# Adding expert outputs in memory with an accumulating scatter, in a fused attention and mixture-of-experts kernel

## The reference, cut to what matters

```
topk_w, topk_ids = grouped_topk(logits, bias)        # 6 of 64 experts a token
buf = zeros(E, CAP + 1, H).at[se, slot].set(x[tok])[:, :CAP]   # CAP = 48
h   = silu(einsum('ech,ehf->ecf', buf, w_gate)) * einsum('ech,ehf->ecf', buf, w_up)
out = einsum('ecf,efh->ech', h, w_down)
gathered = out[se, min(pos, CAP - 1)] * valid[:, None]
y = segment_sum(gathered * w, tok, num_segments=Tn)  # sum of a token's kept expert outputs
```

## Time and profile before

| | us |
|---|---|
| median of 3 runs | 516.87 (515.25 to 517.76) |
| span of the profiled execution | 517.1 |
| token stage, until the first pair's rows are there | 0 to 377 |
| pair stage | 377 to 464 |
| end stage | 464 to 517.1 |

### The profile page before, as it was taken

The page is one execution under the profiler, slowest core; times in us unless marked ns, Lnnn a source line. Parts: engine busy times, 40 slices in busy tenths (PEclk is TensorE's granted clock), DMA queues, the critical chain, the costliest instruction groups (busy, mean ns, idle before and its releaser), DMA issues.

```text
span 517.1 us, 7330 instructions
## 1 busy us (share of the span) xinstructions
PE 309.6 (60%) x2282; PEld 222.4 (43%) x2282; DVE 283.7 (55%) x1066; ACT 98.9 (19%) x253; POOL 212.8 (41%) x310
## 2 busy tenths in 40 slices
PE   0735695968678768859657867150089889940000
PEld 0424484856556556747445655040045444520000
DVE  3550516395194394393393392664067544727995
ACT  1411131413112212303113201000024332430000
POOL 4200112117517527327327237186615433553664
PEclk9958568896786886796787787655579865985555
DMA  7955992963411311311301300000059999119992
GB/s 224 399 183 178 260 317 71 239 214 127 171 35 61 125 47 47 122 41 39 122 20 38 122 22 8 0 5 2 3 153 300 277 270 228 57 38 379 333 323 96
DMA packets 62332, 73.63 MB, mean 142 GB/s; under 512 B 9458, under 2 KB 56955, under 8 KB 62304
## 3 DMA queue, kind: packets, MB, share of 16 engines
q1 hardware_dynamic: 41456, 53.37, 35.2%
q10 hardware_dynamic: 14704, 15.24, 8.4%
q0 software_dynamic: 6144, 4.66, 3.1%
HBM read 48.39 MB, written 40.93 MB: 173 GB/s over the span
## 4 chain that ended last, share of the span: by engine, by line
issue 27%; PE 19%; DVE 16%; POOL 15%; DMA 10%; another core or an unknown queue 5%; ACT 3%; SPq 2%; DVEq 1%; ACTq 0%; POOLq 0%
POOL rows_dram L449 8%; PE ps_s L1268 5%; DVE z L1019 4%; DMA h2row<-rows_dram 2%; DVE scm L821 2%; DMA xa<-in_L_attn_x 2%; DMA scm<-rows_dram 2%; DMA egu<-y_dram 2%; POOL rstd L435 2%; PE ps_o L1166 2%; SPq L300 1%; PE ps_o L1281 1%; PE ps_a L1257 1%; PE ps_c L1281 1%
## 5 line engine op out<-in xcount | busy, mean ns | idle before, releaser
L449 POOL DMA_INDIRECT rows_dram<-h2row,slot_ix x96 | 94.3, 983 | 28.1 <-issue 28.1
L435 POOL TENSOR_TENSOR rstd<-ve,half_exp 128x2 f32<-128x2 f32 x15 | 11.2, 743 | 133.6 <-DVE ve L662 133.4
L1019 DVE TENSOR_REDUCE z<-egu 128x256 f32<-128x1536 f32 x16 | 42.7, 2746 | 10.8 <-DMA egu<-y_dram 10.8
L439 POOL TENSOR_TENSOR pool_pad<-half_exp 128x1 f32<-128x1 f32 x72 | 13.7, 191 | 68.4 <-ACT oT L545 17.0
L821 DVE TENSOR_TENSOR scm<-ps_s,decay 128x2048 f32<-128x2048 f32 x16 | 36.6, 2285 | 4.9 <-PE ps_s L1146 4.9
L1268 PE MATMUL ps_s<-egu,attn 128*64 128x192 f32 x256 | 33.7, 391 | 0.1
L1078 PE MATMUL ps_a<-hT,w_qkv 128*128 128x256 f32 x64 | 24.6, 551 | 11.9 <-ACT hsq L569 7.1
L1174 PE MATMUL ps_a<-ident,h2row 128*128 128x128 f32 x32 | 8.9, 435 | 36.7 <-POOL h2row L473 36.7
L1166 PE MATMUL ps_o<-scm,v_eo 128*32 128x128 f32 x512 | 26.8, 357 | 5.6 <-DVE scm L821 5.6
L827 DVE TENSOR_SCALAR r_den<-r_exp 128x128 f32<-128x128 f32 x8 | 1.8, 230 | 44.0 <-issue 35.0
L545 ACT ACTIVATE h2T<-ps_a 128x512 f32<-128x512 f32 x8 | 4.8, 597 | 105.5 <-PE ps_a L1174 105.5
(11 more groups left out here) (212 smaller groups left out, 725.3 us busy)
## 6 DMA issues: line engine op xcount, KB each, us to landing
y_dram<-y_zeros ACTq DMA_DIRECT2D x8, 1536.0 KB
egu<-y_dram SPq DMA_DIRECT2D x16, 768.0 KB, 5.9
egu<-in_L_ffn_w_gate SPq DMA_DIRECT2D x16, 384.0 KB, 6.7
egu<-in_L_ffn_w_up SPq DMA_DIRECT2D x16, 384.0 KB, 7.9
ed<-in_L_ffn_w_down SPq DMA_DIRECT2D x16, 384.0 KB, 9.7
rows_dram<-scm SPq DMA_DIRECT2D x1, 5376.0 KB, 15.8
mod_b<-mod_dram SPq DMA_DIRECT2D x8, 384.0 KB
h2row<-rows_dram SPq DMA_DIRECT2D x8, 336.0 KB
```

What stands on the lines that cost most here:

```text
L435: g.tensor_tensor(out_, in_, half_exp[:, which], ALU.pow).then_inc(S[done], 1)
L449: g.indirect_dma_start(out=rows_dram, out_offset=bass.IndirectOffsetOnAxis(ap=slot_ix[par][:, tile, j:j + 1], axis=0), in_=h2row[par][:, t ...
L1019: v.tensor_reduce(ysum[m % NT], y_in[m].rearrange("p (j c) -> p c j", c=C), AX_X, ALU.add).then_inc(S["y_sum"], 1)
```

## The change

The table `y_dram` becomes two accumulators of 2048 rows, one for the upper 64 slots of a pair (its first expert) and one for the lower (its second), followed by 128 rows that catch the empty slots. A row of a scatter is added to what the memory holds, so a token's outputs meet in its two rows. Because an addition in memory reads and later writes, each scatter is issued only when the one before it has landed. The row number is now the token's number plus the accumulator's start, with a minimum that sends empty slots to the spare rows. The rest follows: rows of 324 floats, no rank, smaller zeroing, and an end stage with 16 loads of 256 KB on two queues and three DVE instructions a batch.

```diff
-TKEY = KEYS + 8
-ROWW = 336
-YROWS = B * N * TOPK
+TKEY = KEYS
+ROWW = 324
+TOKENS = B * N
+TURNS = 1
+SIDES = 2 * TURNS
+YROWS = 2 * TOKENS
+FAR = 16384
@@ POOL, pair stage @@
-            def put(q, n, w, last_n):
+            def put(q):
+                n = q % OBUF
                 pool.wait_ge(S["put_row"], q + 1)
                 pool.wait_ge(S["e_evac"], q + 1)
                 seen(pool, S["put_step"], q)
                 settle(2).then_inc(S["put_step"], 1)
-                g.indirect_dma_start(out=y_dram, out_offset=bass.IndirectOffsetOnAxis(ap=y_row[w][:, 0:1], axis=0),
-                                     in_=e_out[n], in_offset=None, bounds_check=last_y,
-                                     oob_is_err=False).then_inc(S[f"st_put{n}"], 16)
-                if last_n is not None:
-
-                    pool.wait_ge(S[f"st_put{(n + 1) % OBUF}"], last_n)
+
+                before_it = q - TURNS
+                if before_it >= 0:
+                    pool.wait_ge(S[f"st_put{before_it % OBUF}"], 16 * (before_it // OBUF + 1))
                     pool.sem_inc(S["e_free"], 1)
+                g.indirect_dma_start(out=y_dram[q % TURNS], out_offset=bass.IndirectOffsetOnAxis(ap=y_row[q % WBUF][:, 0:1], axis=0),
+                                     in_=e_out[n], in_offset=None, bounds_check=last_y, oob_is_err=True,
+                                     compute_op=ALU.add).then_inc(S[f"st_put{n}"], 16)
@@ ACT, in each of the first eight token steps @@
-                    a.dma_start(fill_v[s], spread(y_zeros[:], 1, N * TOPK // P)).then_inc(S["st_fill"], 16)
+                    for i in range(TURNS):
+                        a.dma_start(fill_v[i][s], spread(y_zeros[:], 1, 2 * N // P)).then_inc(S["st_fill"], 16)
@@ DVE, pair step @@
-                    v.tensor_tensor(larger[:], xr[x][:, KEYS:TKEY], spread(slot_key[:, q + 1], 1, 8),
-                                    ALU.is_gt).then_inc(S["wcol_ready"], 1)
-                    dve.wait_ge(S["wcol_ready"], q + 2)
-                    v.tensor_reduce(rank[:], larger[:], AX_X, ALU.add).then_inc(S["rank_step"], 1)
-                    dve.wait_ge(S["rank_step"], q + 2)
-                    v.scalar_tensor_tensor(out=y_row[w][:], in0=rank[:], scalar=float(YROWS),
-                                           in1=xr[x][:, TKEY:TKEY + 1], op0=ALU.add,
-                                           op1=ALU.subtract).then_inc(S["put_row"], 1)
+                    last.then_inc(S["wcol_ready"], 1)
+                    v.tensor_scalar(y_row[w][:], xr[x][:, TKEY:TKEY + 1], side_base[:, 0:1], no_token[:, 0:1],
+                                    ALU.add, ALU.min).then_inc(S["put_row"], 1)
@@ SP, end stage @@
-            for t in range(YBUF):
-                load_y(t, t)
...
+            for b in range(0, B, 2):
+                for a in range(SIDES):
+                    sp.dma_start(y_in[b][:, a], y_v[a // 2][a % 2, b]).then_inc(S[f"ld_y{b}"], 16)
+            for b in range(B):
+                sp.wait_ge(S["y_out"], b + 1)
+                sp.dma_start(out_t[b], y_in[b][:, 0]).then_inc(S["st_out"], 16)
@@ ACT, after its last pair step @@
+                for n in range(OBUF):
+                    act.wait_ge(S[f"st_put{n}"], 16 * PAIRS // OBUF)
+                for b in range(1, B, 2):
+                    for i in range(SIDES):
+                        a.dma_start(y_in[b][:, i], y_v[i // 2][i % 2, b]).then_inc(S[f"ld_y{b}"], 16)
@@ DVE, end stage @@
-                    v.tensor_reduce(ysum[m % NT], y_in[m].rearrange("p (j c) -> p c j", c=C), AX_X,
-                                    ALU.add).then_inc(S["y_sum"], 1)
+                v.tensor_tensor(y_in[b][:, 0], y_in[b][:, 0], y_in[b][:, 1], ALU.add).then_inc(S["y_sum"], 1)
+                dve.wait_ge(S["y_sum"], b + 1)
+                v.tensor_tensor(y_in[b][:, 0], y_in[b][:, 0], spread(gb_all[:, b], 1, NT), ALU.mult).then_inc(S["y_gb"], 1)
+                dve.wait_ge(S["y_gb"], b + 1)
+                v.tensor_tensor(y_in[b][:, 0], y_in[b][:, 0], pre[:, NT * b:NT * b + NT], ALU.add).then_inc(S["y_out"], 1)
```

More of the change, by code:

```diff
@@ L73, in adaln_attention_moe @@
         rows_dram = nc.dram_tensor("rows_dram", [ROWS, ROWW], F32, kind="Internal").ap()
-        y_dram = nc.dram_tensor("y_dram", [YROWS, C], F32, kind="Internal").ap()
+        y_dram = [nc.dram_tensor(f"y_dram{i}", [YROWS + P, C], F32, kind="Internal").ap() for i in range(TURNS)]
         mod_dram = nc.dram_tensor("mod_dram", [B, 4 * C], F32, kind="Internal").ap()
@@ L213, in adaln_attention_moe @@
         zeros = scm[:].rearrange("p r j q t -> p (r j q t)")[:, 0:4 * ROWW]
-        y_in = [flat[:, TOPK * C * i:TOPK * C * (i + 1)] for i in range(YBUF)]
-        ysum = [z1[:, i] for i in range(2)]
-        ygb = [h2s[:, i] for i in range(2)]
-        yout = [z2[:, i] for i in range(2)]
+        y_in = [flat[:, SIDES * NT * C * b:SIDES * NT * C * (b + 1)].rearrange("p (a i c) -> p a i c", a=SIDES, c=C)
+                for b in range(min(B, 24 // SIDES))]
         ps_s = ctx.enter_context(nc.psum_tensor("ps_s", [P, 4, 512], F32))
@@ L241, in adaln_attention_moe @@
         xt_taken wcol_ready gup ge_exp gh_ready htp ht_taken dnp e_evac settled put_step put_row
-        rank_step y_sum y_gb y_out
-        """.split() + [f"ld_quad{i}" for i in range(QUADS)]
+        y_sum y_gb y_out
+        """.split() + [f"ld_quad{i}" for i in range(QUADS)] + [f"ld_y{b}" for b in range(B)]
         S = {n: sem(n) for n in names}
@@ L523, in _ @@
-            for i in range(NT):
-                pool.sem_inc(S[f"st_y{i}"], 16)
-            pool.sem_inc(S["settled"], 1)
-            pool.sem_inc(S["y_gb"], NT)
-            with pool.Fori(0, B) as b:
-                for i in range(NT):
-                    gate(NT * b + i, b, i)
+                before_it = q - TURNS
+                if before_it >= 0:
+                    pool.wait_ge(S[f"st_put{before_it % OBUF}"], 16 * (before_it // OBUF + 1))
+                    pool.sem_inc(S["e_free"], 1)
@@ L532, in _ @@
+                g.indirect_dma_start(out=y_dram[q % TURNS], out_offset=bass.IndirectOffsetOnAxis(ap=y_row[q % WBUF][:, 0:1], axis=0),
+                                     in_=e_out[n], in_offset=None, bounds_check=last_y, oob_is_err=True,
+                                     compute_op=ALU.add).then_inc(S[f"st_put{n}"], 16)
+            for q in range(PAIRS):
+                put(q)
         @block.scalar
@@ L640, in _ @@
             pair_steps(act, pair_step)
+            load_y()
         @block.vector
@@ L703, in _ @@
             v.memset(ones_bf[:], 1.0)
+            for half in range(2):
+                v.memset(side_base[SLOTS * half:SLOTS * half + SLOTS], float(FAR + half * TOKENS))
             v.tensor_scalar(part_bit[:], part_ix[:], HD, None, ALU.bitwise_and).then_inc(S["prologue_step"], 1)
@@ L931, in slots @@
                 for i in range(NT):
-                    last = v.max(h2row[par][:, i, KEYS:TKEY], key[:, i])
+                    last = v.max(top_key[:, i], key[:, i])
                 last.then_inc(S["slot_step"], 1)
```

77 lines of the change are left out of this document (23 added, 54 removed).

## The result

The changed kernel took 582.99 us (median of 5 runs, 582.0 to 585.84) against 517.76 us of the kernel before on the same chip: a ratio of 1.125, 95% interval 1.118 to 1.132. The forecast was 533, with a range of 503 to 562. The sign was right; the size was not, and the time lies outside the range. The profiled execution has a span of 584.0 us.

A forecast was written before the change was run, and what follows sets the result against it. It took PE to pace the late pair stage, with DMA engines full early, and DVE to bound the end stage. 517.1 + 44 (pair) - 27.5 (end) - 1 (token) = 532.6, so 533 us, range 503 to 562.

The forecast's parts named there:

- What bounds the kernel: Before: PE paces late pairs, DMA engines are full early, DVE bounds the end; after: scatters should chain the pair stage.
- The end stage: End stage: first load 4.2, DVE 17.3, store 4, so 25.5 us against 53.0, 27.5 us less.
- The token stage: Token stage: zeroing shrinks from 12.6 to 4.2 MB, easing the second batch's input load; 1 us less.
- The pair stage: Pair stage: 32 scatter lives in a row, 123 us against 79.1, so 44 us more.
- POOL's gap before the descriptors after a wait: Pair stage: POOL's pause before each scatter, taken as already inside the 2.37 us life; nothing added.
- The accumulation, +0.6 us: Pair stage: full rows +0.2 and reading the destination +0.39 us per scatter; quiet life 3.0 us; range +0 to +2.0.
- the limit of 1.1 us: Pair stage on POOL: descriptor time above 1.1 us would be a price the forecast left out.
- The rival of a second trip: Pair stage: reading before writing adds 1.4 us per scatter, quiet life 4.4; +85, 573 us in all; chance 0.13.
- The loads, 7.4 lives with 3.8 us more, 28 us: Early pair stage: 50 us of full DMA engines hold 7.4 lives of 6.8 us, the other 24.6 taking 3.0 each.
- Short lives: Pair stage: scatters barely feel loads, a life is 2.6 us; +8, 497 us in all, faster; chance 0.22.
- break-even of 3.36: Pair stage: a mean scatter life of 3.36 us would leave the kernel's time unchanged; chance 0.05 of being near it.
- PE's lower clock: Pair stage: clock stays at 1.2 GHz, quiet pairs take 3.54 us each; +58, 547 us in all; chance 0.15.

The follow-up runs named there:

- e8: Kernel before, its 16 end-stage reductions replaced by three two-operand additions each; 477.1 against 473.71 us.
- e1: Kernel before, each scatter issued only after the landing of the one before it, without addition; 568.85 against 518.64 us.
- e2: Kernel before, its scatters adding to memory, three still under way; 520.83 against 518.64 us.
- e3: Changed kernel with plain scatters in place of adding ones, still each waiting for the last; 545.84 against 518.64 us.
- e4: Changed kernel without the weight loads of the pair stage, pairs 16 to 31 using the weights of 0 to 15; 566.85 against 518.64 us.
- e10: Kernel before, every second tile's six rows summed by PE and copied out by ACT, DVE reducing the others; 476.76 against 476.24 us.
- e11: Kernel before with half of the end sums on PE and four output buffers in place of two; 472.24 against 476.76 us.
- e5: Changed kernel with POOL's increment of `e_free` after the scatter instead of between wait and scatter; 523.0 against 473.71 us.
- e7: Changed kernel with two sets of accumulators, each scatter waiting for the last but one, four rows a token at the end; 479.52 against 473.71 us.
- e9: Changed kernel with two sets of accumulators and POOL's increment of `e_free` after the scatter; 474.13 against 476.24 us.
- e12: Changed kernel unaltered, run again on a third chip; 538.35 against 476.76 us, 1.135.
- e6: Changed kernel with the bound of row numbers lowered so that empty slots are not written; 533.92 against 473.71 us, 1.137.

## Why the prediction was wrong in size

**What bounds the kernel: right.** In the changed kernel the pair stage's chain is scatters, PE is not in its way, and ACT is released by POOL. The end stage is DVE back to back.

**The end stage: right.** 25.5 us predicted, 23.8 measured: SP's issue and the first load 0.5 + 4.2 (predicted 4.2), DVE to 581.4, which is 16.5 us (17.3), the store 2.6 (4). The additions, the groups of that stretch:

```profile
L993 DVE TENSOR_TENSOR egu<-egu,gb_all 128x512 f32<-128x512 f32 x8 | 5.5, 692 | 0.3
...
L991 DVE TENSOR_TENSOR egu<-egu 128x512 f32<-128x512 f32 x8 | 5.5, 685 | 35.5 <-DMA egu<-y_dram 35.5
```

The 0.69 us were of the earlier trace rows, and they hold with POOL idle (e8 shows what becomes of them beside POOL). The loads stay hidden. **The token stage:** 0.7 us less, 1 predicted. That is within the spread of this chip: the first scatter is issued at 383.5 to 385.0 us with the token stage of before (before, e1, e2) and at 381.9 to 384.3 with the new one (after, e3, e4). On the two other chips the gain looks larger, 339.5 to 341.4 (e8, e10, e11) against 335.0 to 335.9 (e5, e7, e9, e12; e6 has 339.8).

**The pair stage: +96.8 us where +44 was said.** The ladder is before 79.1, the order of scatters 131.9 (e1), all rows 137.4 (e3), the addition 175.9. The forecast's own sum is 1 us short, since 24.6 x 3.0 and 7.4 x 6.8 make 124 and not 123; nothing hangs on it. By the terms of the forecast:

1. *"POOL's gap before the descriptors after a wait is in SP's row as its own start, so I add nothing for it."* This step failed. The row of 2.37 us ends with the landing; that SP starts its own load after it says nothing of what POOL needs. POOL needs 0.79 us, in e1 as in the changed kernel, 31 times: 24.5 us. Some 0.57 us of each is the increment that the change puts between wait and scatter (e5). In the kernel before this gap was in no one's way, because no scatter waited for the one before it. The code showed it standing there; I counted what queues behind the scatter, and not what runs ahead of it.

2. *The accumulation, +0.6 us.* It is +1.44: 0.07 for the full rows (0.2 predicted), 0.56 of descriptors (nothing predicted, though the limit of 1.1 us was named), 0.80 of transfer (0.39 predicted). That is 0.84 us x 32 = 27 us more. It was inside the range of 0 to 2.0 that I had bounded; choosing its lower third from packets of a copy was the mistake, because the addition does not keep those packets (143, not 48). The rival of a second trip, 1.4 us in the transfer, gave the nearest time, 573 us, and a quiet life of 4.4. Its number is near for another reason: the life is 3.8, and the rest of the pace is item 1. What makes the 0.80 of transfer is open: 0.83 us more engine time for small packets is as large, but in e6 0.54 of it is gone and a life is only 0.2 us shorter. A second trip is neither needed nor excluded.

3. *The loads, 7.4 lives with 3.8 us more, 28 us.* Measured: 175.9 - 32 x 4.6 = 29 us, 31 in e1 and 33 in e3. The size is right, its form is not, so that it fits is in part luck. I said that the loads fill the same 50 us. They did not: the first 17 intervals take 107.7 us (384.26 to 491.97), 6.3 each, so they lose 1.7 us each on average (lives of 5.2 to 8.3 us mix with others of 3.7 to 4.3). Windows of the changed kernel at such a place and in the quiet part:

```profile
444.00:474.00 30.00, 17.69 (x75) 7.59 (x74) 5.94 (x27) 3.86 (x15) 9.20 (x11) 0.50 0.55 116
500.00:556.00 56.00, 20.17 (x93) 8.16 (x89) 8.10 (x37) 6.99 (x25) 21.40 (x24) 0.56 0.26 29
```

The DMA share is 0.55, not near 1, and the loads come in bursts: SP frees weight buffers by pair, and pairs are slower (argued from the code, not tried). In sum the bursts cost what the forecast had for the full stretch. e4 shows that the late weights are 17 us of it.

Together 24.5 + 27 + 1 account for 52.5 of the 52.8 us by which the pair stage was missed.

The Trainium skill (Collectives: The Full Stack, "Stop ④ — SDMA + CCE: where bytes move and the add happens") calls the addition inside a DMA engine free, a read-read-write in one pass. No run here has such a ring of large slices; of these rows of 1 KB the runs say 1.35 us each when they follow each other, and nothing measurable when three overlap (e2). The rule that the forecast weighed (DMA: Bandwidth & Descriptors of the Trainium skill, "Anatomy of one DMA — SWDGE (gpsimd) path", 2.3 us for 128 KB) fits a copy's life: 2.44 in e3 with all 128 KB, 2.37 in e1 and before with half of them. It did not fit the pace of a chain, 3.16, nor a life beside loads, up to 8.3 us (an addition's) in the chain above.

**The other rivals.** *Short lives*: refuted, since a mean life with its restart is 5.5 us against a break-even of 3.36. *PE's lower clock*: the clock did stay at 0.50, 1.2 GHz, in the first window above, as the rival said. But PE is busy for 17.69 us of 30 there, so it does not set the pace. PE is fully busy only in the first 12 us of this stage (384 to 396, at full clock), while the four output buffers fill.

## What to carry to other kernels

Before a chain of dependent transfers replaces overlapped ones, write down one full cycle on the issuing engine: landing, each instruction between the wait and the issue, descriptors, transfer; the life of a transfer in a chain of waits is only part of it, and an increment that can stand behind the issue should. An accumulating scatter costs little while others overlap it and much alone, so give sums in memory two independent chains: that took the ratio from 1.135 to 1.024 (e7), and with the increment behind the issue to 0.996 [0.991, 1.001] (e9), where a pair stage 18 us longer is paid for by an end stage 15 us shorter. A slower stage spreads its loads over more transfers, but it does not escape them.

## What was not expected of the hardware

- With addition, descriptors for 128 rows take 1.55 us on POOL instead of 1.00 (e3), and the scatter goes in packets of single 1 KB rows: 1.20 us per DMA engine instead of 0.37.
- An increment of a semaphore on POOL between a wait and a scatter costs some 0.57 us (4.59 against 4.02 us apart; e12, e5).
- A DVE addition of 128x256 elements takes 0.43 us when it starts before POOL's instruction of that size, which then takes 0.94 us and not 0.72, and 0.97 when it starts just after one (e8); a reduction of six times the elements is not disturbed (2.75 us, with POOL busy beside it).
- The same program's token stage is 384 us long on one chip and 336 on another (e12), while its pair and end stages agree within 2%.
